# One 128-column weight operand for the adapter's first product, and values without their bias

## The chip, the cores and the metric

The kernel runs on one core of a Trainium2 chip. The metric is the device time of one execution in microseconds (us). A core has TensorE (PE in the profile; its weight loads are PEld), VectorE (DVE), ScalarE (ACT), GpSimd (POOL) and SyncE (SP, which issues most of the DMAs). Each engine runs its own list of instructions in order, and they wait for one another by semaphores. PSUM has eight banks of 128x512 float32 words.

## The reference, cut to what matters

A layer of the macaron kind over a batch of 16 with 512 rows of 256: half a feed-forward block, attention with 16 heads of 16, half a feed-forward block again. In each feed-forward block one of 8 adapters is chosen for each batch, the one whose encoder and decoder rebuild the input best.

```python
# feed-forward, twice for each batch, on x = layernorm(...)
h = relu(einsum('btd,ndh->nbth', x, W_enc) + b_enc)
recon = einsum('nbth,nhd->nbtd', h, W_dec) + b_dec
top1 = argmin(mean((recon - x[None]) ** 2, axis=(2, 3)), axis=0)
adp = connected_idx[top1]
mid = relu(einsum('btd,bdr->btr', x, W_down[adp]) + b_down[adp])   # 256 -> 64
out = x @ W_base + b_base + einsum('btr,brd->btd', mid, W_up[adp]) + b_up[adp]
# attention
q, k, v = x @ Wq + bq, x @ Wk + bk, x @ Wv + bv                    # q and k are rotated
attn = softmax(einsum('bhqd,bhkd->bhqk', q, k) / sqrt(HD))
y = einsum('bhqk,bhkd->bqhd', attn, v).reshape(b, s, D) @ W0 + b0
```

A row of `attn` sums to 1, so a bias on `v` reaches the output as `bv @ W0`, the same for every row.

## The kernel before, in words

Products that need full precision are made from two float32r parts of each operand, a high and a low one: high x high, low x high, high x low, for each of the two 128-row halves `c` of the 256 channels, so six matmuls of 512 columns for one output of 128x512.

The work is a software pipeline over the batches. It is cut into small named stages, and for each engine an order of the stages is written out by hand (`tensor_order`, `scalar_order`, `vector_order`, `gpsimd_order`, `sync_order` for the 13 middle iterations, and a `_begin` and an `_end` for each). In `stage("up", +1, 0, 1)` the numbers are the batch relative to the iteration, the feed-forward block `f` (0 or 1) and a part. In one iteration TensorE computes attention of one batch, and between its pieces the first block of the next batch and the second block of the batches before. The stages that matter here:

- `s1` and `s2` (lines 1680 and 1692): two score matmuls each, into two banks. VectorE takes row maxima of `s1` (line 2076), ScalarE the exponentials of `s2` (line 1919). `pv` (line 1706) multiplies with the values, `nt`, `ot`, `op` (lines 1868, 1876, 1884) finish the attention, `mt` (line 1729) transposes the maxima.
- `tr`, `en`, `gr`, `cost`, `pick`: transposes of the normalised input, the encoder (line 1761, ScalarE's relu in line 1977), the losses (lines 1778 and 1780, VectorE's sum in line 2131; 1789), the choice (VectorE lines 2146 to 2165). GpSimd then copies the chosen weights (lines 2321 to 2326) and counts them on `sel`.
- `dn`: the chosen 256x64 product. TensorE does six matmuls with 64 weight columns (line 1802), ScalarE one relu with the bias (line 1984), counted on `mid_done`.
- `up`: two halves, each twice six matmuls and two with `mid` (lines 1821 and 1822), of which the first waits for `mid_done`. VectorE adds the result to the input (line 2175).
- `qk` and `va`: the projections (lines 1837 and 1847). ScalarE copies queries and keys out with their bias (line 1992), and VectorE the values with theirs (line 2183). Rotation and splitting follow (`ro1`, `ro2`, `ro3` on VectorE, GpSimd and ScalarE), and SyncE sends the parts through HBM into `stack`.

Block 0 of a batch has the banks 6 and 7 (`early`), block 1 the bank 5 (`late`), which it shares with `mt`.

In a middle iteration TensorE's order around the two `dn` is this; block 1's `dn` stands far ahead of its `up`, block 0's close to it:

```python
stage("s2", -1, 14, 0); stage("s1", 0, 3, 0); stage("dn", -2, 1)     # block 1
...
stage("s2", 0, 0, 1); stage("s1", 0, 5, 1); stage("dn", +1, 0)       # block 0
stage("nt", -1, 0); stage("nt", -1, 1)
stage("s2", 0, 1, 0); stage("s1", 0, 6, 0); stage("up", +1, 0, 0)
```

Of the kernel before, what the change touches and what calls it, by code (L numbers as in the profile page):

```python
# [108 lines left out]
def tensor_order(stage):  # L109
# [16 lines left out]
    stage("s1", 0, 2, 0)  # L126
    stage("gr", +1, 0, 0)
# [5 lines left out]
    stage("dn", -2, 1)  # L133
# [9 lines left out]
    stage("cost", +1, 0)  # L143
    stage("s2", -1, 15, 1)
    stage("s1", 0, 4, 1)
    stage("up", -2, 1, 1)
# [16 lines left out]
    stage("s2", 0, 2, 0)  # L163
    stage("ot", -1)
    stage("s1", 0, 7, 0)
# [39 lines left out]
    stage("s2", 0, 7, 1)  # L205
    stage("s1", 0, 12, 1)
    stage("en", -1, 1, 2)
    stage("s2", 0, 8, 0)
    stage("pv", 0, 3)
# [4 lines left out]
    stage("gr", -1, 1, 0)  # L214
    stage("s2", 0, 9, 0)
    stage("tr", +2, 0, 0)
    stage("s1", 0, 14, 0)
    stage("gr", -1, 1, 1)
    stage("s2", 0, 9, 1)
    stage("tr", +2, 0, 1)  # L220
# [11 lines left out]
def tensor_begin(stage):  # L232
# [18 lines left out]
    stage("qk", 0, 0)  # L251
    stage("qk", 0, 1)
    stage("en", 1, 0, 1)
    stage("va", 0, 0)
    stage("va", 0, 1)
    stage("en", 1, 0, 2)
# [10 lines left out]
    stage("s1", 0, 1, 0)  # L267
    stage("dn", 1, 0)
    stage("s1", 0, 1, 1)
    stage("s1", 0, 2, 0)  # L270
    stage("s1", 0, 2, 1)
    stage("up", 1, 0, 0)
    stage("s1", 0, 3, 0)
# [15 lines left out]
    stage("s2", 0, 2, 1)  # L289
    stage("tr", 1, 2, 0)  # L290
    stage("s1", 0, 7, 1)
    stage("s2", 0, 3, 0)
    stage("pv", 0, 0)
    stage("tr", 1, 2, 1)
    stage("mt", 0, 1)
# [3 lines left out]
    stage("s2", 0, 4, 0)  # L299
    stage("s1", 0, 9, 0)  # L300
    stage("pv", 0, 1)
    stage("s2", 0, 4, 1)
    stage("s1", 0, 9, 1)
    stage("qk", 1, 0)
    stage("s2", 0, 5, 0)
    stage("s1", 0, 10, 0)
    stage("qk", 1, 1)
    stage("s2", 0, 5, 1)
    stage("s1", 0, 10, 1)
    stage("s2", 0, 6, 0)  # L310
    stage("va", 1, 0)
    stage("s1", 0, 11, 0)
    stage("pv", 0, 2)
    stage("s2", 0, 6, 1)
    stage("s1", 0, 11, 1)
    stage("va", 1, 1)
    stage("s2", 0, 7, 0)
    stage("s1", 0, 12, 0)
    stage("qk", 1, 2)
    stage("mt", 0, 2)  # L320
    stage("s2", 0, 7, 1)
    stage("qk", 1, 3)
    stage("s1", 0, 12, 1)
    stage("pv", 0, 3)
    stage("s2", 0, 8, 0)
    stage("s1", 0, 13, 0)
    stage("s2", 0, 8, 1)
# [7 lines left out]
    stage("tr", 2, 0, 0)  # L335
    stage("s2", 0, 10, 1)
    stage("s1", 0, 15, 1)
    stage("tr", 2, 0, 1)
# [3 lines left out]
def tensor_end(stage):  # L342

    stage("en", -1, 0, 0)
    stage("mt", -3, 3)
    stage("s2", -3, 11, 0)
# [5 lines left out]
    stage("s2", -3, 12, 0)  # L352
    stage("pv", -3, 5)
    stage("s1", -2, 1, 0)
# [4 lines left out]
    stage("s1", -2, 2, 0)  # L359
    stage("s2", -3, 13, 1)  # L360
    stage("gr", -1, 0, 0)
    stage("s1", -2, 2, 1)
    stage("s2", -3, 14, 0)
    stage("gr", -1, 0, 1)
    stage("s1", -2, 3, 0)
    stage("dn", -4, 1)
    stage("s2", -3, 14, 1)
    stage("s1", -2, 3, 1)
    stage("gr", -1, 0, 2)
    stage("gr", -1, 0, 3)  # L370
    stage("mt", -2, 0)
    stage("pv", -3, 6)
    stage("s2", -3, 15, 0)
    stage("s1", -2, 4, 0)
    stage("up", -4, 1, 0)
    stage("cost", -1, 0)
    stage("s2", -3, 15, 1)
# [3 lines left out]
    stage("s2", -2, 0, 1)  # L381
    stage("pv", -3, 7)
    stage("s1", -2, 5, 1)
    stage("up", -4, 1, 1)
    stage("dn", -1, 0)
    stage("nt", -3, 0)
    stage("nt", -3, 1)
    stage("s2", -2, 1, 0)
    stage("s1", -2, 6, 0)
    stage("up", -1, 0, 0)  # L390
    stage("nt", -3, 2)
    stage("s2", -2, 1, 1)
    stage("nt", -3, 3)
    stage("s1", -2, 6, 1)
    stage("s2", -2, 2, 0)
    stage("up", -1, 0, 1)
# [21 lines left out]
    stage("s1", -2, 9, 1)  # L418
    stage("tr", -3, 1, 1)
    stage("s2", -2, 5, 0)  # L420
# [7 lines left out]
    stage("s2", -2, 6, 1)  # L428
    stage("s1", -2, 11, 1)
    stage("qk", -1, 2)  # L430
    stage("en", -3, 1, 0)
    stage("s2", -2, 7, 0)
    stage("pv", -2, 2)
    stage("s1", -2, 12, 0)
    stage("mt", -2, 2)
    stage("qk", -1, 3)
    stage("s2", -2, 7, 1)
    stage("s1", -2, 12, 1)
    stage("en", -3, 1, 1)
    stage("pv", -2, 3)  # L440
    stage("s2", -2, 8, 0)
    stage("en", -3, 1, 2)
    stage("s1", -2, 13, 0)
    stage("s2", -2, 8, 1)
    stage("en", -3, 1, 3)
    stage("s1", -2, 13, 1)
    stage("s2", -2, 9, 0)
    stage("gr", -3, 1, 0)
# [3 lines left out]
    stage("s1", -2, 14, 1)  # L452
    stage("s2", -2, 10, 0)
    stage("s1", -2, 15, 0)
    stage("gr", -3, 1, 2)
    stage("s2", -2, 10, 1)
    stage("pv", -2, 4)
# [16 lines left out]
    stage("dn", -3, 1)  # L474
    stage("s1", -1, 2, 1)
    stage("s2", -2, 14, 0)
    stage("s1", -1, 3, 0)
    stage("s2", -2, 14, 1)
    stage("s1", -1, 3, 1)
    stage("pv", -2, 6)  # L480
    stage("s2", -2, 15, 0)
    stage("s1", -1, 4, 0)
    stage("mt", -1, 0)
    stage("s2", -2, 15, 1)
    stage("up", -3, 1, 0)
    stage("s1", -1, 4, 1)
    stage("pv", -2, 7)
    stage("up", -3, 1, 1)
    stage("s2", -1, 0, 0)
    stage("s1", -1, 5, 0)  # L490
    stage("nt", -2, 0)
    stage("s2", -1, 0, 1)
    stage("nt", -2, 1)
    stage("s1", -1, 5, 1)
    stage("nt", -2, 2)
    stage("nt", -2, 3)
    stage("s2", -1, 1, 0)
    stage("s1", -1, 6, 0)
    stage("s2", -1, 1, 1)
    stage("s1", -1, 6, 1)  # L500
    stage("s2", -1, 2, 0)
    stage("ot", -2)
    stage("s1", -1, 7, 0)
    stage("pv", -1, 0)
# [4 lines left out]
    stage("op", -2, 1)  # L509
    stage("s1", -1, 8, 0)  # L510
    stage("s2", -1, 3, 1)
    stage("mt", -1, 1)
# [13 lines left out]
    stage("s1", -1, 11, 1)  # L526
    stage("pv", -1, 2)
    stage("s2", -1, 7, 0)
    stage("s1", -1, 12, 0)
    stage("mt", -1, 2)  # L530
    stage("s2", -1, 7, 1)
    stage("s1", -1, 12, 1)
    stage("pv", -1, 3)
# [211 lines left out]


def scalar_end(stage):

    stage("en", -1, 0, 0)
    stage("s2", -3, 11, 0)  # L750
    stage("s2", -3, 11, 1)
# [1612 lines left out]
```

## Time and profile before

| | |
|---|---|
| median of 3 runs | 1786.44 us (1784.21 to 1788.15) |
| the profiled execution | 1784.44 us |
| its span, first to last instruction | 1782.6 us |
| mean granted TensorE clock | 0.988 of full speed |
| PE, DVE, ACT, POOL busy | 1703.6, 1265.2, 973.0, 497.0 us |

The span is 1.8 us shorter than the execution's own time. Matmuls overlap one another in the records: one of 512 columns is shown as some 390 ns long, while the next starts about 230 ns after it. So the cost of a group of matmuls is read from the chain of waits, where pieces follow end to end, and not from the mean of one.

### The profile page before, as it was taken

Reading aid. Unit: us, or ns where it says so; the run is one execution under the profiler, and the core shown is the slowest. Engines: PE = TensorE matmul, PEld = TensorE weight load, DVE = VectorE, ACT = ScalarE, POOL = GpSimd, SP = SyncE. Lnnn points to the kernel's source line nnn. Section 1 sums busy time; section 2 is a strip of 40 time slices with the busy share of each in tenths; the row PEclk is TensorE's granted clock in tenths of the full one; section 3 lists DMA queues with packets and bytes.
Section 4 is the critical chain, followed back from the end, with each engine's and each line's share of the span. In section 5 each row is a group of like instructions: output and inputs, shape, how many; then the busy total and the mean of one; then the engine's idle time right before and its main releaser. Section 6 shows DMA issues by size and latency. Waiting matters only on the chain.

```text
span 1782.6 us, 26353 instructions
## 1 busy us (share of the span) xinstructions
PE 1703.6 (96%) x9064; PEld 997.6 (56%) x9064; DVE 1265.2 (71%) x2829; ACT 973.0 (55%) x1954; POOL 497.0 (28%) x663
## 2 busy tenths in 40 slices
PE   5878999999999999999999999999999999999987
PEld 4624555556565565656556565655656565554345
DVE  6478786867768686776868677686867868576722
ACT  2326474655637465563746556474655647465551
POOL 2314060421406042140604215060421506023010
PEclk9889999999999999999999999999999999999999
DMA  5343342223334222343422234332233434224300
GB/s 133 48 71 72 37 82 32 62 40 60 72 49 79 35 61 42 61 72 48 76 36 62 43 61 72 48 75 36 61 45 60 72 48 75 32 33 70 44 1 24
DMA packets 96715, 99.37 MB, mean 56 GB/s; under 512 B 19972, under 2 KB 88261, under 8 KB 96453
## 3 DMA queue, kind: packets, MB, share of 16 engines
q1 hardware_dynamic: 93830, 97.16, 32.6%
q8 instruction: 72, 1.18, 0.3%
q10 hardware_dynamic: 2752, 0.54, 0.2%
q14 instruction: 61, 0.50, 0.1%
HBM read 63.54 MB, written 33.55 MB: 54 GB/s over the span
## 4 chain that ended last, share of the span: by engine, by line
PE 84%; DVE 8%; ACT 2%; issue 2%; POOL 2%; DMA 1%; SPq 0%; POOLq 0%; ACTq 0%; DVEq 0%
PE ps L1706 11%; PE ps L1692 11%; PE ps L1680 11%; PE ps L1778 10%; PE ps L1761 10%; PE ps L1780 6%; PE ps L1821 5%; PE ps L1837 5%; PE ps L1822 3%; PE ps L1802 3%; PE ps L1745 2%; PE ps L1847 2%; DVE mx L2076 2%; PE ps L1884 2%; PE ps L1868 2%
## 5 line engine op out<-in xcount | busy, mean ns | idle before, releaser
L2076 DVE TENSOR_REDUCE mx<-ps 128x1 f32<-128x512 f32 x1024 | 655.5, 683 | 258.8 <-PE ps L1680 257.6
L1919 ACT ACTIVATE pr<-ps 128x512 f32<-128x512 f32 x1024 | 557.3, 599 | 386.5 <-PE ps L1692 383.0
L1680 PE MATMUL ps<-stack 96*128 96x512 bf16 x1024 | 316.0, 384 | 12.4 <-DVE mx L2076 8.5
L1692 PE MATMUL ps<-stack 98*128 98x512 bf16 x1024 | 314.6, 384 | 9.2 <-ACT pr L1919 3.3
L1706 PE MATMUL ps<-pr,va 128*32 128x512 f32 x2048 | 247.7, 602 | 2.6 <-ACT pr L1919 2.3
L1692 PEld LDWEIGHTS ps<-stack 98*128 98x128 bf16 x1024 | 82.4, 98 | 184.5 <-issue 106.9
L1680 PEld LDWEIGHTS ps<-stack 96*128 96x128 bf16 x1024 | 95.2, 98 | 156.0 <-DVE mx L2076 50.9
L2321 POOL CAST wdh<-wd_all 128x128 fp32r x32 | 9.5, 297 | 585.2 <-DVE adapter L2165 557.4
L2131 DVE SCALAR_TENSOR_TENSOR ps<-ps,wb,h 128x512 f32<-128x512 f32 x128 | 96.5, 755 | 65.1 <-PE ps L1780 65.1
L1780 PE MATMUL ps<-h,gram_w 128*128 128x512 f32 x256 | 130.6, 592 | 0.0
L1706 PEld LDWEIGHTS ps<-pr,va 128*32 128x32 f32 x2048 | 53.7, 109 | 136.2 <-issue 131.2
L1778 PE MATMUL ps<-xh,w_dh 128*128 128x512 f32 x256 | 121.5, 475 | 6.8 <-DVE ps L2131 4.4
L1761 PE MATMUL ps<-xh,w_eh 128*128 128x512 f32 x256 | 123.6, 483 | 0.9 <-DVE xl L2118 0.9
L2248 POOL TENSOR_SCALAR rs<-mv 128x4 f32<-128x4 f32 x48 | 11.4, 237 | 404.7 <-DVE mv L2096 399.6
L1977 ACT ACTIVATE h<-ps,benc 128x512 f32<-128x512 f32 x128 | 87.1, 693 | 64.1 <-PE ps L1761 64.0
L2277 POOL TENSOR_TENSOR qb<-qb,cst 128x512 f32<-128x512 f32 x64 | 91.4, 1428 | 47.4 <-DVE qs L2191 46.9
L1761 PE MATMUL ps<-xl,w_eh 128*128 128x512 f32 x256 | 101.8, 398 | 0.0
L1761 PE MATMUL ps<-xh,w_el 128*128 128x512 f32 x256 | 101.6, 397 | 0.0
L1778 PE MATMUL ps<-xl,w_dh 128*128 128x512 f32 x256 | 101.2, 395 | 0.0
L1778 PE MATMUL ps<-xh,w_dl 128*128 128x512 f32 x256 | 101.1, 395 | 0.0
L2285 POOL TENSOR_TENSOR qb<-qb,parts 128x512 f32<-128x512 f32 x64 | 78.9, 1233 | 79.0 <-ACT parts L1998 79.0
L1821 PE MATMUL ps<-w_bh,xh 128*128 128x256 f32 x256 | 96.4, 376 | 1.5 <-ACT mid L1984 1.5
(153 smaller groups left out, 2951.5 us busy)
## 6 DMA issues: line engine op xcount, KB each, us to landing
stack<-scratch SPq DMA_DIRECT2D x384, 128.0 KB, 6.3
scratch<-parts SPq DMA_DIRECT2D x64, 384.0 KB, 2.6
xin<-in_L_attn_x_dram SPq DMA_DIRECT2D x15, 512.0 KB, 4.0
out_dram<-x SPq DMA_DIRECT2D x15, 512.0 KB, 8.8
stack<-wu_mT SPq DMA_DIRECT2D x128, 4.0 KB, 1.7
cst<-in_const_dram SPq DMA_DIRECT2D x1, 1024.0 KB
raw<-in_L_ffn_W_dec_dram ACTq DMA_DIRECT2D x1, 512.0 KB, 5.6
pr<-in_L_ffn_W_enc_dram SPq DMA_DIRECT2D x2, 256.0 KB, 7.6
```

What stands on the lines that cost most here:

```text
L1680: pe.matmul(bank1[:, t % 2, :], stack[0][0:KB, hd, 128 * t:128 * t + 128], stack[1][0:KB, hd, :], start=True, stop=True).then_inc(s1_full. ...
L1692: pe.matmul(bank2[:, a % 2, :], stack[1][:, 4 * g + a, 128 * t:128 * t + 128], stack[0][:, 4 * g + a, :], start=True, stop=True).then_inc( ...
L1706: last = pe.matmul(bank_o[32 * a:32 * a + 32, :], va[b.odd][:, t, 4 * g + a, :], held(b, n)[:, a, :], start=(t == 0), stop=(t == T - 1))
L1761: last = pe.matmul(bank, w[:, c, 2 * p:2 * p + 2, :].rearrange("p n r -> p (n r)"), x[e][:, c, :], start=(c == 0 and w is w_eh and x is xh ...
L1778: pe.matmul(bank, w[:, c, 128 * p:128 * p + 128], x[e][:, c, :], start=(c == 0 and w is w_dh and x is xh), stop=False)
L1780: pe.matmul(bank, gram_w[:, p, :], h[:, p, :], start=False, stop=True).then_inc(gr_full[f].sem, 1)
L1821: pe.matmul(o, x[e][:, c, 128 * t:128 * t + 128], w[:, c, :], start=(c == 0 and n == 0), stop=False)
L1837: last = pe.matmul(bank, y[:, c, 128 * m:128 * m + 128], x[:, c, :], start=(c == 0 and n == 0), stop=(c == C - 1 and n == 2))
L1919: act.activation(held(b, n)[:, a, :], bank2[:, a % 2, :], ACT.Exp, scale=SCALE).then_inc(ex_done.sem, 1)
L2076: dve.tensor_reduce(mx[:, hd // 4 % 2, e:e + 1], bank1[:, t % 2, :], AX.X, ALU.max).then_inc(mx_done.sem, 1)
L2131: dve.scalar_tensor_tensor(out=bank, in0=bank, scalar=wb2[:, p:p + 1], in1=h[:, p, :], op0=ALU.add, op1=ALU.mult, accum_out=r[e][:, p:p + ...
L2277: pool.tensor_tensor(q[:], q[:], v["cos"][:, S * (k // 2):S * (k // 2) + S], ALU.mult).then_inc(cos_done.sem, 1)
```

## The change

1. `dn`: the high and the low part of the chosen weights lie side by side in one tile `wd`, 128 columns wide. TensorE multiplies it with the high and the low part of the input: four matmuls of 128 columns in place of six of 64. Rows 0 to 63 of the bank then hold the high weights' sum, rows 64 to 127 that of the low weights.
2. The two halves have to be added. ScalarE copies rows 64 to 127 into `mid` (stage `dn`), VectorE adds both and the bias into the bank (a new stage `dn`), and ScalarE does the relu into `mid` (a new stage `ds`).
3. `va`: ScalarE copies the values out, without a bias. Once, at the start, TensorE computes `bv @ W0` (two float32 matmuls of 256 columns ahead of the first `qk`), and VectorE adds it to `b0`. The broadcast load of `bv` becomes two loads of a column.
4. All orders are written anew. Most moves are by one or two places.

```diff
@@ tensor_order (middle iterations)
     stage("s1", 0, 2, 0)
+    stage("dn", -2, 1)
     stage("gr", +1, 0, 0)
...
     stage("s1", 0, 3, 0)
-    stage("dn", -2, 1)
...
     stage("up", -2, 1, 0)
-    stage("cost", +1, 0)
     stage("s2", -1, 15, 1)
     stage("s1", 0, 4, 1)
+    stage("cost", +1, 0)
...
     stage("dn", +1, 0)
+    stage("s2", 0, 1, 0)
+    stage("s1", 0, 6, 0)
     stage("nt", -1, 0)
     stage("nt", -1, 1)
-    stage("s2", 0, 1, 0)
-    stage("s1", 0, 6, 0)
     stage("up", +1, 0, 0)
@@ tensor_end
     stage("op", -1, 1)
     stage("gr", -2, 1, 0)
     stage("gr", -2, 1, 1)
+    stage("tr", -1, 1, 0)
     stage("gr", -2, 1, 2)
-    stage("tr", -1, 1, 0)
     stage("tr", -1, 1, 1)
     stage("gr", -2, 1, 3)
+    stage("en", -1, 1, 0)
     stage("cost", -2, 1)
-    stage("en", -1, 1, 0)
     stage("en", -1, 1, 1)
+    stage("en", -1, 1, 2)
     stage("dn", -2, 1)
-    stage("en", -1, 1, 2)
+    stage("en", -1, 1, 3)
     stage("up", -2, 1, 0)
-    stage("en", -1, 1, 3)
-    stage("up", -2, 1, 1)
@@ scalar_order
+    stage("dn", -2, 1)
     stage("s2", -1, 14, 0)
     stage("pv", -1, 5)
-    stage("dn", -2, 1)
     stage("s2", -1, 14, 1)
+    stage("ds", -2, 1)
...
     stage("s2", 0, 0, 1)
     stage("dn", +1, 0)
+    stage("ds", +1, 0)
     stage("s2", 0, 1, 0)
...
+    stage("ro2", +1, 0)
     stage("tr", -1, 1, 1)
-    stage("ro2", +1, 0)
     stage("s2", 0, 6, 0)
+    stage("va", +1, 0)
     stage("s2", 0, 6, 1)
+    stage("va", +1, 1)
     stage("ro3", +1, 0)
@@ vector_order
+    stage("gr", +1, 0, 2)
+    stage("dn", -2, 1)
     stage("s1", 0, 3, 1)
-    stage("gr", +1, 0, 2)
...
     stage("s1", 0, 5, 1)
+    stage("dn", +1, 0)
     stage("nt", -1, 0)
...
     stage("ro1", +1, 1)
-    stage("va", +1, 0)
     stage("s1", 0, 11, 0)
     stage("s1", 0, 11, 1)
     stage("ms", 0, 2)
-    stage("va", +1, 1)
@@ vector_end
     stage("s1", -2, 6, 0)
+    stage("dn", -1, 0)
     stage("nt", -3, 0)
@@ tensor: down
-                    for w, x in ((wdh, xh), (wdl, xh), (wdh, xl)):
-                        last = pe.matmul(bank[0:R, :], w[e][:, c, :], x[e][:, c, :], ...)
+                    for x in (xh, xl):
+                        last = pe.matmul(bank, wd[e][:, c, :, :].rearrange("p k r -> p (k r)"), x[e][:, c, :], ...)
@@ tensor: project
+                if initial(b) and k == 0:
+                    for c in range(C):
+                        last = pe.matmul(bank_o[:, 0:D], bv_col[:, c:c + 1].to_broadcast([128, 128]), w_0[:, c, :], ...)
+                    last.then_inc(s_wt, 1)
@@ scalar
-                act.activation(mid[e][0:R, :], bank[0:R, :], ACT.Relu, bias=bdn[e][:, 0:1]).then_inc(mid_done[f].sem, 1)
+                act.copy(mid[e][0:R, :], bank[R:2 * R, :]).then_inc(rest_mid[f].sem, 1)
+            def middle_sum(b, f):
+                act.wait_ge(*sum_mid[f].at(b, 0))
+                act.activation(mid[e][0:R, :], bank[0:R, :], ACT.Relu).then_inc(mid_done[f].sem, 1)
+            def values(b, half):
+                act.wait_ge(*va_full.at(b, half))
+                act.copy(va[b.odd][:, 2 * half:2 * half + 2, :, 0:HD], bank...).then_inc(va_done.sem, 1)
@@ vector
+            def down(b, f):
+                dve.wait_ge(*rest_mid[f].at(b, 0))
+                dve.wait_ge(*sel[f].at(b, 1))
+                dve.scalar_tensor_tensor(out=bank[0:R, :], in0=bank[0:R, :], scalar=bdn[e][:, 0:1], in1=mid[e][0:R, :],
+                                         op0=ALU.add, op1=ALU.add).then_inc(sum_mid[f].sem, 1)
-            def values(b, half):   # a tensor_tensor with the broadcast bias
@@ vector: swap, before the first
+                    dve.wait_ge(s_wt, 3)
+                    dve.tensor_tensor(b0_bc[:], b0_bc[:], bank_o[:, 0:D], ALU.add).then_inc(s_ready, 1)
```

## Rows read from the trace of the kernel before

**Rows 1.** The page: busy time by engine, and the chain's shares.

```profile
PE 1703.6 (96%) x9064; PEld 997.6 (56%) x9064; DVE 1265.2 (71%) x2829; ACT 973.0 (55%) x1954; POOL 497.0 (28%) x663
...
PE 84%; DVE 8%; ACT 2%; issue 2%; POOL 2%; DMA 1%; SPq 0%; POOLq 0%; ACTq 0%; DVEq 0%
```

**Rows 2.** Windows: one middle iteration of 104 us.

```profile
core 0: us, PE busy (x) PEld busy (x) DVE busy (x) ACT busy (x) POOL busy (x), PEclk, DMA share, GB/s
...
832.00:936.00 104.00, 103.50 (x566) 61.64 (x565) 77.82 (x174) 60.46 (x122) 30.66 (x41) 1.00 0.33 55
```

**Rows 3.** Chain of waits, 809 to 831 us: start, us, what.

```profile
809.51 1.40 PE ps L1778 x6
...
827.17 1.37 PE ps L1802 x6
828.54 0.87 PE ps L1868 x8
...
830.28 0.71 PE ps L1821 x6
```

**Rows 4.** Instruction groups: busy us, mean ns, idle before.

```profile
L1928 ACT COPY raw<-ps 128x512 f32<-128x512 f32 x64 | 38.3, 599 | 27.7 <-PE ps L1706 27.7
...
L1984 ACT ACTIVATE mid<-ps,bdn 64x512 f32<-64x512 f32 x32 | 21.8, 682 | 75.8 <-PE ps L1802 75.8
L2183 DVE TENSOR_TENSOR va<-ps,bv_bc 128x512 f32<-128x512 f32 x32 | 21.8, 683 | 0.3 <-PE ps L1847 0.3
...
L2175 DVE SCALAR_TENSOR_TENSOR x<-ps,xin 128x512 f32<-128x512 f32 x30 | 20.7, 691 | 30.4 <-PE ps L1822 30.4
```

**Rows 5.** Timelines of ScalarE, VectorE and GpSimd around block 0's `dn`.

```profile
826.75 1.09 ACT L1919 ACTIVATE pr<-ps 128x512 f32<-128x512 f32 x2
828.58 0.68 ACT L1984 ACTIVATE mid<-ps,bdn 64x512 f32<-64x512 f32 x1 [0.74 <-PE ps L1802]
...
826.99 1.29 DVE L2076 TENSOR_REDUCE mx<-ps 128x1 f32<-128x512 f32 x2 [1.54 <-PE ps L1680]
...
825.11 0.39 POOL L2326 COPY wu_mT<-wu_all 65x256 f32 x1
```

**Rows 6.** Chain of waits: the last `dn`.

```profile
1770.10 2.84 PE ps L1802 x6
1772.96 0.69 ACT mid L1984
1773.70 0.98 PE ps L1821 x6
```

**Rows 7.** Instruction groups: weight loads of 64 and of 128 columns.

```profile
L1761 PEld LDWEIGHTS ps<-xh,w_eh 128*128 128x128 f32 x256 | 48.5, 189 | 21.4 <-DVE xl L2118 1.3 <-ACT h L1977 0.9
...
L1802 PEld LDWEIGHTS ps<-xh,wdh 128*64 128x64 f32 x64 | 9.0, 141 | 15.8 <-issue 5.2 <-POOL wu_mT L2326 4.9
```

**Rows 8.** Chain of waits, the first `dn`.

```profile
40.63 2.81 PE ps L1802 x6
43.46 0.69 ACT mid L1984
```

**Rows 9.** Chain of waits in the end: float32 matmuls, and `dn` of batch 14.

```profile
1666.71 1.73 PE ps L1884 x8
...
1746.97 1.59 PE ps L1802 x6
```

**Rows 10.** Waits of the whole run: us in total, times, longest.

```profile
PE ps L1789 <- DVE z L2140: 4.0, 3, 1.4
```

**Rows 11.** Windows and timeline where ScalarE would copy the values.

```profile
855.00:860.00 5.00, 5.00 (x36) 3.97 (x35) 3.79 (x6) 5.00 (x14) 3.31 (x3) 1.00 0.00 0
...
863.52 1.09 ACT L1919 ACTIVATE pr<-ps 128x512 f32<-128x512 f32 x2 [0.91 <-PE ps L1692]
```

**Rows 12.** Waits between 780 and 884 us: TensorE's weight loads for VectorE.

```profile
PEld ps L1680 <- DVE mx L2076: 0.8, 1, 0.8
PEld ps L1778 <- DVE ps L2131: 0.5, 1, 0.5
```

More of the change, by code:

```diff
@@ L827, in scalar_end @@
     stage("s2", -2, 14, 1)
+    stage("dn", -3, 1)
+    stage("ds", -3, 1)
     stage("s2", -2, 15, 0)
@@ L1463, in macaron @@
         zt = [sb(f"zt{f}", [128, C, N]) for f in range(2)]
-        wdh, wdl = ([sb(f"{n}{f}", [128, C, R], FR) for f in range(2)] for n in ("wdh", "wdl"))
+        wd = [sb(f"wd{f}", [128, C, 2, R], FR) for f in range(2)]
         wu_mT = [sb(f"wu_mT{f}", [128, D]) for f in range(2)]
@@ L1555, in macaron @@
         mid_done = [sig(f"mid_done{f}", 1) for f in range(2)]
+        rest_mid = [sig(f"rest_mid{f}", 1) for f in range(2)]
+        sum_mid = [sig(f"sum_mid{f}", 1) for f in range(2)]
         up_done = [sig(f"up_done{f}", 2) for f in range(2)]
@@ L1800, in down @@
                 for c in range(C):
-                    for w, x in ((wdh, xh), (wdl, xh), (wdh, xl)):
-                        last = pe.matmul(bank[0:R, :], w[e][:, c, :], x[e][:, c, :], start=(c == 0 and w is wdh and x is xh),
-                                         stop=(c == C - 1 and x is xl))
+                    for x in (xh, xl):
+                        last = pe.matmul(bank, wd[e][:, c, :, :].rearrange("p k r -> p (k r)"), x[e][:, c, :],
+                                         start=(c == 0 and x is xh), stop=(c == C - 1 and x is xl))
                 last.then_inc(dn_full[f].sem, 1)
@@ L1833, in project @@
                     pe.wait_ge(*va_done.at(b, k - 2))
+                if initial(b) and k == 0:
+                    for c in range(C):
+                        last = pe.matmul(bank_o[:, 0:D], bv_col[:, c:c + 1].to_broadcast([128, 128]), w_0[:, c, :], start=(c == 0),
+                                         stop=(c == C - 1))
+                    last.then_inc(s_wt, 1)
                 w, m = (w_q, w_k)[k % 2], k // 2
@@ L1993, in project @@
                    .then_inc(qb_done.sem, 1)
+            def values(b, half):
+                if half == 0:
+                    act.wait_ge(*pv_done.at(b - 2, G * T // 2 - 1))
+                bank = early[half]
+                act.wait_ge(*va_full.at(b, half))
+                act.copy(va[b.odd][:, 2 * half:2 * half + 2, :, 0:HD], bank.rearrange("p (t h d) -> p t h d", t=2, d=HD))\
+                   .then_inc(va_done.sem, 1)
             def high(b, k):
@@ L2008, in out_transposed @@
                     act.copy(oT[:, c, :], out_bank(b, c)).then_inc(oT_done.sem, 1)
-            do = dict(s2=s2, pv=pv, mt=maxima, lx=normalise, tr=transposed, en=encode, dn=down, qk=project,
+            do = dict(s2=s2, pv=pv, mt=maxima, lx=normalise, tr=transposed, en=encode, dn=down, ds=middle_sum, qk=project, va=values,
                            ro2=high, ro3=middle, ot=out_transposed)
@@ L2167, in choose @@
                     dense_weights()
+            def down(b, f):
+                e = slot(b, f)
+                bank = dense_bank(b, f, 1)
+                dve.wait_ge(*rest_mid[f].at(b, 0))
+                dve.wait_ge(*sel[f].at(b, 1))
+                dve.scalar_tensor_tensor(out=bank[0:R, :], in0=bank[0:R, :], scalar=bdn[e][:, 0:1], in1=mid[e][0:R, :], op0=ALU.add,
+                                         op1=ALU.add).then_inc(sum_mid[f].sem, 1)
             def up(b, f, half):
@@ L2176, in up @@
                                          in1=src[:, q, :], op0=ALU.mult, op1=ALU.add).then_inc(up_done[f].sem, 1)
[L2178 to L2185 removed]
             def swap(b, k):
+                if initial(b) and k == 0:
+                    dve.wait_ge(s_wt, 3)
+                    dve.tensor_tensor(b0_bc[:], b0_bc[:], bank_o[:, 0:D], ALU.add).then_inc(s_ready, 1)
                 dve.wait_ge(*qb_done.at(b, k))
@@ L2223, in out_project @@
                    .then_inc(x2_done.sem, 1)
-            do = dict(s1=s1, ms=split_maxima, st=statistics, lx=normalise, tl=low_part, gr=gram, cost=cost, pick=choose, up=up, va=values,
-                           ro1=swap, ro3=low, nt=natural,
+            do = dict(s1=s1, ms=split_maxima, st=statistics, lx=normalise, tl=low_part, gr=gram, cost=cost, pick=choose, dn=down, up=up, ro1=swap, ro3=low, nt=natural,
                            op=out_project)
```

350 lines of the change are left out of this document (180 added, 170 removed).

## The prediction

> **What bounds the kernel now.** I read the page first. TensorE is busy for 96% of the span and makes up 84% of the chain that ended last, while VectorE is at 71% and ScalarE at 55% [rows 1]. That is an average, so I asked for windows. In a middle iteration TensorE is busy for 103.5 of 104 us, VectorE for 77.8 and ScalarE for 60.5 [rows 2]: there TensorE is the bound, and a matmul less shortens the run by its own spacing, unless TensorE then waits. The spacing has to come from the chain of waits, since the mean of one matmul counts overlap. Six matmuls of `dn` take 1.37 us there and six of 128 columns 1.40, so 0.233 each [rows 3].
>
> **What TensorE saves.** Four matmuls of 0.233 us in place of six that take 1.37: 1.37 - 0.93 = 0.44 us for each of the 32 `dn`. The rest is what else changes around each.
>
> The width costs nothing in that sum, since a load of 128 columns takes 189 ns against 141 [rows 7], under the spacing of 233. The Trainium skill, page TensorE: Matmul & The Clock Gate, section LDWEIGHTS, says that a load's time goes with its columns, and its section Back-to-back issue gap that the spacing is set by load and matmul together. If they simply added up, its figures would give, as an estimate, 6 x (0.216 + 0.053) - 4 x (0.216 + 0.107) = 0.32 us saved in place of 0.44. The trace speaks against adding: twice the columns move the spacing by 4 ns.
>
> **What the halves' sum costs.** Before, `dn` is followed by one relu: it starts 0.04 us after the product's end, takes 0.68 [rows 5], and TensorE can go on 0.05 later [rows 6]. Afterwards there are three steps on two engines: copy on ScalarE, 0.58 (128x512 copies average 0.60 [rows 4]; a lone one is a little shorter), sum on VectorE, 0.69 like line 2175 [rows 4], relu without a bias pointer, 0.60 like the exponentials, of which a pair takes 1.09 [rows 5]. With hand-overs of 0.04, 0.05 and 0.04 that is 2.00 us from the product's end to `mid_done`. No row shows a 64x512 copy from one half of the partitions to the other. From below: if half the rows were to halve each step, 0.29 + 0.35 + 0.30 and the hand-overs make 1.07. From above: each of the three as long as the longest of these rows, 0.69, and 0.15 for each hand-over make 2.5. I take the 2.00, since the old relu on 64 rows took 682 ns, no less than line 2183's sum on 128, so half the rows halve nothing.
>
> Block 1's `dn` has all four `gr` of the next batch behind it before `mt` and `up` need the bank or `mid` (each of them over 1.40 us [rows 3]), and its copy and its relu are put behind work that TensorE does not wait for. So it keeps its 0.44 us. There are 14 of these, batches 0 to 13, in the middle and in the first part of the end: **-6.2 us**. On VectorE the added sum (0.69) and the removed value copies (0.68 each, two for each batch [rows 4]) cancel, since there are two `dn` for each batch.
>
> Block 0's `dn` has little cover. From its end to the first matmul of `up` TensorE does `nt` twice, `s2` and `s1`: 828.54 to 830.28, 1.74 us [rows 3]. The new order permutes these four and has the same 1.74. Before, the 0.77 of the relu lay inside. Afterwards `mid` comes at 2.00, and a matmul that had to wait starts late on top: six of line 1821 take 0.98 us behind such a wait [rows 6] and 0.71 without [rows 3]; with the 0.05 that is 0.32. So TensorE stands still for 2.00 + 0.32 - 1.74 = 0.58 us. Neither engine is late for it: ScalarE's exponentials end at 827.84 and VectorE's maxima at 828.28 [rows 5], while they are wanted from 828.1 and 828.7 (0.44 earlier than `dn` ended before). ScalarE's next exponentials stand behind its relu, and end some 1.1 us after it, while TensorE has half of `up` to do before it needs them, twice 0.71 [rows 3] and the products with `mid`. The chosen weights are there at 825.50 [rows 5], over a us early. So for each of the 13 middle batches 0.58 - 0.44 = +0.14: **+1.8 us**. What block 1 saves, block 0 does not.
>
> Batch 15's block 0, in the end, is worse: there VectorE's order has the two maxima of the `s1` behind `dn` ahead of its sum. They take 1.29 us [rows 5] and can begin some 0.2 after the product's end, so the sum starts 0.8 later than its copy allows, and the stall is about 1.4: 1.4 - 0.44, **+1.0**.
>
> **Start and end.** At the first `dn` nothing covers anything. Six matmuls at the lower clock took 2.81 us with their drain [rows 8], or 0.43 each, so two less save 0.85; the chain behind grows by 2.00 - 0.72 = 1.28. `bv @ W0` stands ahead of the first `qk`: a float32 matmul of 256 columns is spaced 1.73 / 8 = 0.22 [rows 9], twice that at the lower clock, so two cost 0.86. Together **+1.3**. Batch 1's `dn` lies where row maxima bind: -0.85 on TensorE against +0.69 on VectorE, **-0.2**. The two small loads of `bv` I cost at nothing: they stand among the other first loads, and the first `dn`, which waits for the chosen weights, is 40 us away [rows 8]; without that cover they would cost what a queue step takes, well under a us.
>
> In the end, `cost` of batch 14 waited 1.4 us for VectorE [rows 10], and the new order puts an encoder product of 1.40 in there; behind it `dn` still waits for the weights, which come at 1746.97 [rows 9], and `up` then waits for the longer chain, some 0.5 more. The work from there to batch 15's `cost` comes 1.4 - 0.5 earlier: **-0.9**. The last `dn` is bare again: 2.84 / 6 x 2 = 0.95 saved, 1.28 added, **+0.35**.
>
> Sum: -6.2 + 1.8 + 1.0 + 1.3 - 0.2 - 0.9 + 0.35 = **-2.8 us**. The profiled execution took 1784.44 us, 1.8 more than its span, and stands 2.0 below the median of the runs. So 1781.6 for an execution like it, and 1783.6 for the median.
>
> **Rivals.**
> *All hidden.* If the three short steps are near their lower bound, TensorE does not stop in block 0: 13 x 0.58 less, -10.3, 1776. Half the partitions speak for it; the relu's 682 ns on 64 against 599 and more on 128 speaks against.
> *ScalarE becomes the bound where it copies values.* It is busy for 5.00 of 5 us from 855 to 860, and its exponentials have 0.91 us of air only at 863.5 [rows 11]. Two copies of 0.5 to 0.6 fill that, and `s2` needs the banks that they delay. If 0.7 us of the 1.1 reach TensorE in each of 13 iterations, +9.3: 1793, slower. It decides from some 0.5 us for each iteration. Against it: the air of 0.91 us lies just where the first copy goes, and a value copy on ScalarE ends over 2 us before `qk` asks for its bank.
> *VectorE, relieved, stops holding TensorE.* In an iteration the weight loads wait 0.8 us for maxima and 0.5 for the gram's sum [rows 12]. 1.4 us less of value copies where VectorE is busiest could free some 0.4 of it: -5.2, 1778.
> *The narrow product was not dearer.* If four wide matmuls cost nearly what six narrow ones did, by loads that show, the 27 savings in the middle shrink. With 0.12 less each: +3.2, so +0.4, 1787. The rule cited above would lead here. Rows 3 and 7 speak against.
>
> **Numbers.** Forecast 0.45, with a range of its own from 1780 to 1787 (the stall between 0.35 and 0.85 us); all hidden 0.15; ScalarE 0.17; VectorE 0.13; no saving by width 0.10. 0.2% of 1786.4 is 3.6 us, about what a measurement of this kernel tells from no change. Faster, under 1782.9: 0.16 of the forecast's, all of the hidden, 0.12 of VectorE's, 0.43. Slower, over 1790.0: 0.14 of ScalarE's and 0.02 beside, 0.16. Within: 0.41. The range goes from 1775.5, which takes in the lower bound of the chain, to 1791.
>
> **What would show it.** Line 1802's successor: 128 matmuls in fours of 0.93 us. TensorE waiting some 0.4 us, as the records count it, for `mid` ahead of line 1821's block 0, in each middle iteration, and a middle iteration some 0.3 us shorter. If `s2` waits for ScalarE beyond 860, or the waits for maxima are gone, it was a rival. I am wrong if ScalarE's copy or relu takes much less than 0.58, or if one of them comes up behind an exponential.

## The result, and the profile after

The changed kernel takes 1795.89 us (median of 5 runs, 1792.22 to 1797.88) against 1786.44 (5 runs, 1784.02 to 1788.49): ratio 1.0059, 95% interval [1.0048, 1.0071]. It is slower by about 10 us, where 3 us less was forecast.

The page of the kernel after, which answers to [rows 1]:

```profile
PE 1706.9 (95%) x9004; PEld 998.8 (56%) x9004; DVE 1279.5 (71%) x2830; ACT 1010.4 (56%) x2018; POOL 494.1 (28%) x663
...
PE 73%; DVE 16%; ACT 5%; issue 3%; POOL 3%; DMA 1%; POOLq 0%; ACTq 0%; DVEq 0%; SPq 0%
```

The busy shares hardly move. The chain does: TensorE's part falls from 84% to 73%, VectorE's doubles to 16%. Something on VectorE is now late for TensorE.

The chain of waits around block 0's `dn` in a middle iteration, which answers to [rows 3]:

```profile
833.56 0.94 PE ps L1824 x4
834.50 0.02 issue
834.52 0.59 ACT mid L2010
835.11 0.03 issue
835.14 0.76 DVE ps L2214
835.90 0.02 issue
835.92 0.60 ACT mid L2016
836.52 0.04 issue
836.57 0.98 PE ps L1843 x6
```

The four wide products take 0.94 us, and `mid` comes 2.02 us behind them. That is the forecast, almost to the hundredth (0.93 and 2.00). So the loss is elsewhere.

To find it I use one measure in all that follows: the **distance**, from one batch's first score product to the next batch's. Each batch has 64 of them, so the first is every 64th record of that line. The timelines of before and after at batches 3 and 7:

```profile
375.24 0.60 PE L1680 MATMUL ps<-stack 96*128 96x512 bf16 x2
791.62 0.60 PE L1680 MATMUL ps<-stack 96*128 96x512 bf16 x2
```

```profile
380.08 0.60 PE L1700 MATMUL ps<-stack 96*128 96x512 bf16 x2
798.41 0.60 PE L1700 MATMUL ps<-stack 96*128 96x512 bf16 x2
```

A quarter of the difference is 104.10 us before and 104.58 after. The eleven distances from batch 2 to batch 13 agree within 0.1 us but for one or two (their median: 104.09 and 104.60), so a tenth of a microsecond can be read there, where whole runs scatter by several. The 11.5 us between the two spans are made up so: up to batch 1's first scores 3.4, from there to batch 2's 1.1, batches 2 to 13 4.9, 13 to 14 1.9, 14 to 15 -0.5, the rest 0.6.

Where VectorE is late, about 85 us into such an iteration, its timeline after:

```profile
883.37 1.28 DVE L2116 TENSOR_REDUCE mx<-ps 128x1 f32<-128x512 f32 x2
884.57 2.57 DVE L2149 SCALAR_TENSOR_TENSOR xn<-xin,mv,rs 128x256 f32<-128x256 f32 x4
887.06 1.28 DVE L2116 TENSOR_REDUCE mx<-ps 128x1 f32<-128x512 f32 x2
888.26 0.74 DVE L2171 SCALAR_TENSOR_TENSOR ps<-ps,wb,h 128x512 f32<-128x512 f32 x1
```

And the same place before:

```profile
876.88 1.66 DVE L2109 SCALAR_TENSOR_TENSOR xn<-xin,mv,rs 128x256 f32<-128x256 f32 x4
```

The four operations that normalise the next batch, `lx(+2,0)`, took 1.66 us before and take 2.57 after, though nothing in them was changed, and VectorE has no idle time right behind them in which to catch up. GpSimd at that time, after and before:

```profile
885.43 1.42 POOL L2328 TENSOR_TENSOR qb<-qb,parts 128x512 f32<-128x512 f32 x1 [1.70 <-ACT parts L2038]
```

```profile
878.57 1.17 POOL L2285 TENSOR_TENSOR qb<-qb,parts 128x512 f32<-128x512 f32 x1 [2.51 <-ACT parts L1998]
```

The waits of TensorE's weight loads for VectorE in that iteration, which answer to [rows 12]:

```profile
PEld ps L1700 <- DVE mx L2116: 1.9, 4, 0.8
...
PEld ps L1800 <- DVE ps L2171: 1.2, 2, 0.6
```

That is 3.1 us where it was 1.3. As to what changed: before, GpSimd's subtraction for the third rotated projection, its stage `ro2(+1,2)`, starts when the four have ended. After, it starts in the middle of them. It waits for ScalarE's copy, the stage of the same name there, here after and before:

```profile
884.75 0.61 ACT L2038 CAST parts<-qb 128x512 bf16<-128x512 f32 x1
```

```profile
877.89 0.61 ACT L1998 CAST parts<-qb 128x512 bf16<-128x512 f32 x1
```

Counted from the iteration's first score product (798.41 and 791.62), that copy starts at the same time in both, 86.3 us. It is VectorE that comes to its four operations 0.9 us later, at 86.2 in place of 85.3.

### The profile page after: what moved, and what is told of

Read it like the earlier page. It is cut to its first block, busy times and chain, and to the rows that moved or that the text cites. A ratio compares the mean times of both kernels' runs of the same rounds, so it can differ in the third digit from the quotient of the medians.

```text
span 1794.1 us, 26301 instructions
## 1 busy us (share of the span) xinstructions
PE 1706.9 (95%) x9004; PEld 998.8 (56%) x9004; DVE 1279.5 (71%) x2830; ACT 1010.4 (56%) x2018; POOL 494.1 (28%) x663
## 4 chain that ended last, share of the span: by engine, by line
PE 73%; DVE 16%; ACT 5%; issue 3%; POOL 3%; DMA 1%; POOLq 0%; ACTq 0%; DVEq 0%; SPq 0%
PE ps L1728 10%; PE ps L1800 9%; PE ps L1712 9%; PE ps L1700 9%; PE ps L1783 7%; PE ps L1843 6%; PE ps L1802 5%; DVE mx L2116 5%; PE ps L1864 4%; PE ps L1844 3%; DVE xn L2149 3%; PE ps L1874 2%; PE ps L1767 2%; PE ps L1824 2%; ACT pr L1946 2%
## 5 line engine op out<-in xcount | busy, mean ns | idle before, releaser
L1700 PE MATMUL ps<-stack 96*128 96x512 bf16 x1024 | 320.4, 385 | 10.8 <-DVE mx L2116 8.7
L2364 POOL CAST wd<-wd_all 128x128 fp32r x32 | 9.5, 296 | 570.9 <-DVE adapter L2205 434.5
L2320 POOL TENSOR_TENSOR qb<-qb,cst 128x512 f32<-128x512 f32 x64 | 100.9, 1576 | 140.4 <-DVE qs L2233 140.4
```

What stands on the lines that cost most here:

```text
L1700: pe.matmul(bank1[:, t % 2, :], stack[0][0:KB, hd, 128 * t:128 * t + 128], stack[1][0:KB, hd, :], start=True, stop=True).then_inc(s1_full. ...
L2320: pool.tensor_tensor(q[:], q[:], v["cos"][:, S * (k // 2):S * (k // 2) + S], ALU.mult).then_inc(cos_done.sem, 1)
```

## The experiments

Each is compared with the kernel before, run beside it on the same chip. The ratio comes from all its runs; the distance (within 0.02 us of the median over batches 2 to 13) and the start of batch 1's first score product come from one profiled execution each.

| kernel | distance, us | batch 1's first scores at, us | ratio to before, 95% interval |
|---|---|---|---|
| before | 104.09 | 171.7 | |
| changed | 104.58 | 175.1 | 1.0059 [1.0048, 1.0071] |
| down projection alone | 103.80 | 179.5 | 1.0033 [1.0019, 1.0047] |
| values alone | 104.00 | 177.6 | 1.0019 [1.0007, 1.0032] |
| orders alone | 104.97 | 174.4 | 1.0060 [1.0042, 1.0077] |
| changed, `ro2(+1,1)` first | 104.54 | 171.1 | 1.0032 [1.0018, 1.0046] |
| both parts, old orders | 103.75 | 175.6 | 1.0048 [1.0036, 1.0060] |
| the same, other bank | 103.20 | 181.4 | 1.0004 [0.9992, 1.0015] |
| changed, two copies first | 104.52 | 171.0 | 1.0051 [1.0038, 1.0064] |
| before, two copies late | 104.77 | 176.0 | 1.0050 [1.0037, 1.0063] |
| other bank, new start | 103.20 | 177.3 | 0.9980 [0.9971, 0.9990] |
| changed, copies and encoder | 103.94 | 171.1 | 0.9983 [0.9973, 0.9993] |
| changed, `ro2(+1,2)` later | 103.94 | 172.6 | 0.9974 [0.9962, 0.9987] |
| before, encoder early | 105.53 | 169.4 | 1.0108 [1.0087, 1.0128] |
| changed, later, other bank | 103.41 | 172.4 | 0.9949 [0.9932, 0.9967] |
| other bank, new start and end | 103.20 | 170.9 | 0.9929 [0.9911, 0.9948] |
| before, `ro2(+1,2)` later | 104.09 | 178.6 | 1.0002 [0.9986, 1.0017] |

### Taking the change apart

The down projection alone: the new functions for `dn` and `ds` in the kernel before, the new steps put into its orders at their places, as

```
     stage("s1", 0, 3, 1)
+    stage("dn", -2, 1)      # VectorE
...
     stage("dn", +1, 0)
+    stage("ds", +1, 0)      # ScalarE
```

> The kernel before with the new down projection alone (four 128-column products, the low half copied by ScalarE, the sum on VectorE, the ReLU on ScalarE), the values left on VectorE and the order of the kernel before kept but for the new steps. Theory A, that the new orders hold the loss and the arithmetic does not: the iteration gains 0.87 us of TensorE work and loses 0.6 us at block 0's up projection, 0.2 to 0.3 us for each of 13 batches, against 1 to 2 us at the start and the end, so 1783 to 1787 us (ratio 0.998 to 1.000). Theory B, that the two new VectorE and ScalarE steps themselves delay the maxima and the exponentials: +0.4 us or more for each batch, 1791 us or more (ratio over 1.003).

The values alone: ScalarE's copies put ahead of and behind `s2(0,6,1)`, the bias by way of the output bias.

> The kernel before with the value part alone: values copied by ScalarE, the value bias taken through the output bias, the old down projection and the old order but for the two copies. Theory A: only the start pays (the product of the value bias with W0, 1.6 us, and the wait of the third projection for ScalarE's copy), so +1 to +4 us, 1787 to 1790 us. Theory B, that ScalarE becomes late with its other copies through the two value copies and drags the low parts on GpSimd and VectorE: +0.5 to +0.8 us in each of 13 iterations as well, 1794 to 1799 us.

The orders alone: the new orders, without their new steps, over the old functions.

> The arithmetic of the kernel before (six 64-column products, one ReLU, values on VectorE) walked in the orders of the changed kernel, with VectorE's value steps at their old neighbours. Theory A: the orders alone bring the 0.8 us for each of 13 iterations that the trace of the changed kernel shows ahead of the second decoder's products and at the maxima, so +6 to +11 us, 1792 to 1798 us. Theory B, that the loss comes with the new operations and not with where the stages stand: within 2 us of the kernel before.

Measured: distances of 103.80, 104.00 and 104.97. The down projection gains 0.29 us in an iteration and the values 0.09; the orders lose 0.88, the same sum as the 0.49 by which the changed kernel is longer (0.88 - 0.29 - 0.09 = 0.50). Theory A holds for the iteration. It missed the time of the first kernel, though (1792.75 us, where it had up to 1787), and the second, at 1790.1, is at its upper end: both are slower than before. In their traces batch 1's first scores come 7.8 and 5.9 us later than before, and the stretch from batch 15's first scores to the end is 5.0 and 2.2 us longer (159.7 and 156.8 in place of 154.7). So both ends of the run pay; see the clock below.

Both parts in the old orders, all new steps where the first two kernels have them:

> Both parts of the change (the new down projection and the values on ScalarE) in the orders of the kernel before, with the new steps put in at their places. The three runs so far put 0.88 us of a middle iteration on the orders, 0.30 us of gain on the down projection and 0.08 us of gain on the values. If these add up (theory A), the distance between the scores of two batches is 103.7 us (before 104.09, changed 104.57) and 13 iterations gain 5 us against the kernel before; the start costs 3 to 8 us, by how long TensorE is granted half the clock between 90 and 130 us, so 1785 to 1790 us (ratio 1.000 to 1.002). If the parts disturb each other (theory B), the distance is 104.1 us or more and the time 1793 us or more.

103.75: it adds up. The time, 1793.2 us, does not follow: in the trace the start costs 3.9 us and the stretch behind batch 15's first scores 4.8.

### What in the orders

The first suspicion was one line of ScalarE's order:

```
+    stage("ro2", +1, 1)
     stage("s2", 0, 7, 0)
-    stage("ro2", +1, 1)
```

> The changed kernel with one line moved: ScalarE's first-part copy of the second rotated projection, ro2(+1,1), stands ahead of s2(0,7,0) again as it did before, not behind it. Theory A: that late copy pushes GpSimd's rotation work onto VectorE's four normalising operations, which slow from 0.41 us to 0.64 us each beside it and make VectorE late for the second decoder; with the copy back, 0.5 to 0.8 us for each of 13 iterations return, so 6 to 10 us under the changed kernel: ratio to the kernel before 1.000 to 1.003. Theory B, that the delay has another source (the value copies, or the new steps): the ratio stays at 1.005 to 1.007.

The distance is 104.54: this theory, as put, fell. The run as a whole was 4 us shorter, but that is its start, and who looks at the ratio alone is misled. Its trace has the four operations at 2.58 us still, and VectorE waiting 1.2 us for `ro3(+1,1)`, the next copy. So:

```
+    stage("ro2", +1, 1)
     stage("s2", 0, 7, 0)
-    stage("ro2", +1, 1)
     stage("qk", +1, 2)
+    stage("ro3", +1, 1)
     stage("en", -1, 1, 1)
-    stage("ro3", +1, 1)
```

> The changed kernel with two lines of ScalarE's order moved back: ro2(+1,1) ahead of s2(0,7,0), and ro3(+1,1) ahead of en(-1,1,1). Moving the first alone left the iteration at 104.55 us, and the trace of it still has VectorE wait 1.2 us for ScalarE's second-part copy, ro3(+1,1), which stands behind the encoder step. Theory A: that copy is what is late; GpSimd's rotation then falls on VectorE's four normalising operations (2.6 us in place of 1.7), and with the copy back the wait of the second decoder's products for VectorE (0.46 us more than before) goes: 104.0 to 104.2 us for each iteration, 5 to 7 us off the changed kernel's iterations. Theory B, that the place of TensorE's and VectorE's stages does it: it stays at 104.5 us.

104.52: still not. But the opposite, the kernel before with these two lines as the changed one has them, is slower at once:

> The kernel before with only those two lines of ScalarE's order as the changed kernel has them: ro2(+1,1) behind s2(0,7,0), ro3(+1,1) behind en(-1,1,1). Theory A: the wait and the slower normalising operations appear in the kernel before as well, and its iteration goes from 104.09 to 104.4 or more, so 4 us or more, 1790 us. Theory B: it stays within 0.1 us of 104.09.

104.77, and the mean of the normalising operation goes from 474 to 670 ns (692 in the changed kernel). The group of it in this kernel:

```profile
L2109 DVE SCALAR_TENSOR_TENSOR xn<-xin,mv,rs 128x256 f32<-128x256 f32 x60 | 36.7, 670 | 1.8 <-POOL rs L2250 1.8
```

These two lines are enough to make the loss, and not enough to take it away: there is a second cause with the same effect. In the trace of the changed kernel with both copies first, VectorE waits for TensorE ahead of the maxima of `s1(0,12,1)`, since the new order has `en(-1,1,2)` in front of it. Moving that as well:

```
-    stage("en", -1, 1, 2)
     stage("s1", 0, 12, 1)
-    stage("pv", 0, 3)
+    stage("en", -1, 1, 2)
     stage("s2", 0, 8, 0)
+    stage("pv", 0, 3)
```

> The changed kernel with ScalarE's ro2(+1,1) and ro3(+1,1) ahead as before, and on TensorE the third encoder product en(-1,1,2) behind s1(0,12,1) again and pv(0,3) behind s2(0,8,0). With ScalarE's two alone the iteration stayed at 104.51 us, and VectorE's maximum of s1(0,12,1) came 0.9 us later than in the kernel before, after a wait for TensorE. Theory A, that either of the two delays alone is enough to put the four normalising operations beside GpSimd's subtraction: now the operations take 1.7 us again, the wait of the second decoder's products goes, and the iteration is 104.0 to 104.2 us. Theory B: 104.4 us or more.

103.94, the operations at 478 ns again, and 1782.6 us. Whether TensorE's two lines alone would have done it in the changed kernel was not tried. In the kernel before, the encoder's move alone (with `pv`) does something else:

> The kernel before with two stages of TensorE's order as the changed kernel has them: en(-1,1,2) ahead of s1(0,12,1), and pv(0,3) ahead of s2(0,8,0). Theory A, that this too makes VectorE late enough for the slow normalising operations: 104.4 to 104.8 us for an iteration in place of 104.09. Theory B: within 0.1 us of 104.09.

105.53, but with the normalising operations at 478 ns: theory A was wrong about how. There ScalarE's copy `ro2(+1,2)` is late too: it starts at 885.65, when the four operations (883.98, 1.66 us) are over. What costs is that `en(-1,1,3)` waits 1.7 us for ScalarE's `h`, which is behind exponentials whose scores TensorE, in this order, delivers later. Out of the waits of one iteration of it:

```profile
PEld ps L1761 <- ACT h L1977: 1.7, 1, 1.7
```

A stage moved in one engine's order alone can cost more than the whole change.

### The collision by itself

If the loss is that GpSimd's subtraction and VectorE's four operations fall together, then it must help to make the subtraction later. In the changed kernel, one line of ScalarE's order:

```
-    stage("ro2", +1, 2)
     stage("s2", 0, 8, 1)
+    stage("ro2", +1, 2)
```

> The changed kernel with one copy of ScalarE made later: the first part of the third rotated projection, ro2(+1,2), stands behind the exponentials of s2(0,8,1) and not ahead of them, so GpSimd's subtraction that waits for it starts some 1.1 us later. Theory A, that VectorE's four normalising operations are slow (2.6 us in place of 1.7) because they run beside that subtraction: they end before it starts and take 1.7 to 2.0 us, the wait of the second decoder's products shrinks, and the iteration falls from 104.57 us to 104.1 to 104.3 although an operation was delayed. Theory B, that the delay of VectorE's queue has nothing to do with GpSimd: nothing gained, 104.6 us or more.

VectorE and GpSimd in its trace:

```profile
878.22 1.66 DVE L2149 SCALAR_TENSOR_TENSOR xn<-xin,mv,rs 128x256 f32<-128x256 f32 x4
```

```profile
880.07 1.16 POOL L2328 TENSOR_TENSOR qb<-qb,parts 128x512 f32<-128x512 f32 x1 [2.68 <-ACT parts L2038]
```

The four end at 879.88 and the subtraction starts at 880.07. They take 1.66 us, the distance is 103.94, and the kernel takes 1782.35 us, 13.5 under the changed one, though nothing but one copy was made later. Between the two traces the span is 13.4 us shorter. The distances give 9.2 of that (6.9 from batch 2 to 13, 0.6 ahead of them, 1.7 between 13 and 14). The rest is where nothing was touched: 2.5 up to batch 1's first scores and 1.7 behind batch 15's. It could be that the move is good in itself; so the kernel before, which has no such collision, with the same move:

> The kernel before with the same single move, ro2(+1,2) behind s2(0,8,1). In it the four normalising operations already end before GpSimd's subtraction starts and take 1.7 us. Theory A, that the move helps only where the two fall together: no gain, 104.1 us for an iteration (or up to 0.1 more), 1785 to 1787 us. Theory B, that the move gives something of its own, and the changed kernel's gain of 13.5 us by it says nothing of a collision: 103.5 us or less, 1779 us or less.

104.09, and 1.0002. The move gives nothing where there is nothing to part.

How the two engines meet shows in one answer for the four operations after:

```profile
L2149 DVE SCALAR_TENSOR_TENSOR xn<-xin,mv,rs x4: 473/478/1385, 884.6 to 885.7; 128x256 f32<-128x256 f32 x4
```

Three take their usual 473 to 478 ns. Only the last, which starts at 885.75 while the subtraction runs from 885.43 to 886.85, takes 1385: it ends 0.28 us after the subtraction does. So it is in each of the 13 middle iterations: it ends 0.28 to 0.29 us after the subtraction. That is an operation held up until the other ends, not one slowed all along. The subtraction is longer too, 1.42 us in place of 1.17; it started inside the third of the four. The Trainium skill, page SBUF — State Buffer, section Who interferes with whom, says this: a VectorE instruction with two inputs in SBUF and a GpSimd instruction that reads SBUF take the same ports, the one that starts first has them for its whole length, and the other stands still. The trace agrees: this operation reads `xin` and `rs` there, both in SBUF, and GpSimd's subtraction had started 0.32 us ahead of it. The maxima that follow, with one input and that from PSUM, run beside GpSimd's next operation in their usual 1.28 us for two.

### The wait that was forecast, taken away

Block 0's `dn` filled the bank that `up` fills next, so `up` could not start ahead of `mid`. The output accumulator's bank is free at that time:

```
+            return dense_bank(b, f, 1) if f or initial(b) else bank_o
...
+                if not f:
+                    pe.wait_ge(*raw_done.at(b - 2, G - 1))
...
+                    if t == 0 and not (f or initial(b)):
+                        pe.wait_ge(*mid_done[f].at(b, 0))
                     last = pe.matmul(o, mid[e][:, 128 * t:128 * t + 128], wu[e], start=False, stop=True)
```

> The kernel of both parts in the old orders, with block 0's down projection of every batch but the first written into the output accumulator's bank, which is free there, in place of the bank that the up projection fills; so the up projection starts its twelve base products at once and waits for the ReLU only ahead of its first product with the hidden layer. Theory A, that the 0.6 us stall at the up projection is the price of the added sum: it goes, the distance between batches falls from 103.7 to 103.1 us, 13 iterations give 8 us, 1777 to 1783 us (ratio 0.995 to 0.999). Theory B, that the time is set there by VectorE's or ScalarE's exponentials and maxima and the stall is only where TensorE shows it: the distance stays at 103.6 us or more.

103.20 in place of 103.75: the 0.59 us wait goes, nearly whole, and 1793.2 us become 1785.8. This is level with before only. Its trace, one of its longest runs (1790.98 us), gains 11.8 us from batch 1 to batch 14 and loses 9.7 ahead of that and 8.7 behind batch 15's first scores. The start first, with the changed kernel's orders:

> The kernel with both parts in the old orders and block 0's down projection in the output accumulator's bank, its start walked in the changed kernel's orders. With the old start TensorE was granted half the clock for 30.7 us on end from about 91 to 97 us (kernels of the values alone, of both parts, and of this bank); the changed kernel's start had 6.8 and 10.2 us in its trace. Theory A, that the order of the start decides this: the second batch's scores start at 171 to 175 us and not at 182, the iterations stay at 103.2 us, so 1775 to 1781 us, faster than both kernels (ratio 0.995 to 0.998). Theory B, that chance decides it (the kernel before has runs at 1784 and at 1791 us): the same 1786 us as with the old start, give or take 3.

1782.2, between the two ranges: the start gives some of it. With the changed kernel's orders of the end, which cover the last three batches, as well:

> The kernel with both parts, the down projection in the output accumulator's bank, and the middle iterations in the order of the kernel before, now with the changed kernel's orders for both the start and the end. With the old end orders it took 1782.2 us although its iterations were 103.2 us; from the last score to the end of the span it took 74.5 us against 71.6 us where the changed kernel's end order is used. Theory A, that the end order I made by putting the new steps into the old one costs this: 3 to 5 us less, 1777 to 1780 us. Theory B, that the difference is the clock's: no change beyond 1 us.

1773.0 us, 9 less; more than either theory gave. In the two traces it is 1.2 us between batch 14's and batch 15's first scores and 8.5 from there to the end of the span (163.9 against 155.4). (The traces also differ by 6.5 us up to batch 1's first scores, though the start is the same code: the first of them is the longest of its 12 runs.) So the orders of the end that I had made by putting new steps into the old ones did cost several microseconds, and the changed kernel's own end was the better one. In part it may be the clock again: behind batch 15's first scores TensorE has half of it for 22.8 us against 15.9; which of the two brought the other is not shown. And the other way to it, the changed kernel with both repairs:

> The changed kernel with ro2(+1,2) behind s2(0,8,1) and block 0's down projection in the output accumulator's bank, the up projection waiting for the hidden layer only ahead of its first product with it. With the first alone the iteration is 103.94 us, of which 0.59 us is the up projection's wait. Theory A, that the two losses (VectorE's operations beside GpSimd, and the wait that the sum brings) are independent: 103.3 to 103.4 us for an iteration, 13 times 0.6 us under the 1782.4 us of the first alone, so 1773 to 1777 us (ratio 0.993 to 0.996). Theory B, that the work only queues up at the next limit (VectorE's maxima): 103.7 us or more and 1779 us or more.

103.41 and 1775.0 us: the two losses are independent. This kernel and the one above it are faster than the kernel before by 0.5% and 0.7%.

### The start and TensorE's clock

Windows of 4 us in the kernel before, where TensorE waits for the first projections to come back through memory, and starts the scores (the column behind POOL is the granted clock):

```profile
88.00:92.00 4.00, 0.64 (x3) 0.14 (x2) 2.32 (x11) 0.00 (x0) 0.00 (x0) 0.82 1.15 136
...
96.00:100.00 4.00, 4.00 (x10) 1.51 (x9) 1.57 (x4) 0.67 (x2) 0.35 (x1) 0.50 0.00 0
...
104.00:108.00 4.00, 2.84 (x18) 1.88 (x17) 2.87 (x5) 0.00 (x0) 0.07 (x1) 1.00 0.00 0
```

And in the kernel with the values alone:

```profile
88.00:92.00 4.00, 1.16 (x5) 0.26 (x4) 2.48 (x12) 0.00 (x0) 0.00 (x0) 1.00 0.98 171
...
104.00:108.00 4.00, 3.47 (x12) 1.93 (x10) 1.71 (x3) 0.00 (x0) 0.00 (x0) 0.50 0.00 0
...
116.00:120.00 4.00, 2.84 (x7) 0.52 (x7) 3.39 (x8) 1.09 (x2) 0.50 (x1) 0.50 0.78 134
```

In both the clock falls to half, 1.2 GHz, after TensorE was busy for little of 4 us, 0.64 and 1.16. Before, it is back at 2.4 by 104 us; with the values alone it is at half from 93.5 to 124.2. From batch 0's first scores to batch 1's the kernel before takes 78.9 us and this one 85.8. The kernel before does it too, at times: 7 of its 29 runs beside the first four experiments took over 1790 us, at a mean clock of 0.981 to 0.983, where most of the others took 1783 to 1786 at 0.988 to 0.990. All 12 runs of the down projection alone had 0.978 to 0.982. The kernel before with `ro2(+1,2)` later shows what such a run looks like: its trace is of one that took 1792.45 us, its distances are those of before, and it is 6.9 us longer from batch 0's first scores to batch 1's, with the clock at half from 90.7 to 124.8 us. So the parts put into the old start nearly always end up in the longer case: three of the four traces with new parts in it take over 85 us there, one 82.2. The nine traces with the changed kernel's start take 79.0 to 82.1; why was not tried.

## Why the prediction was wrong, step by step

- **What TensorE saves** (0.44 us for each `dn`): right, 0.94 us for four.
- **The chain of the halves' sum** (2.00 us): right, 2.02. Copy 0.58 and relu 0.59 on average as forecast, the sum 0.75 in place of 0.69.
- **Block 0's stall** (0.58): right, 0.59 (0.32 idle, and 0.27 by which the six products behind the wait take longer, 0.98 against 0.71); TensorE's work between the two ends was the same in the new order. With it fell the rival in which all is hidden, and with the 0.94 the one in which the width costs.
- **A middle iteration 0.3 us shorter**: right for the arithmetic, by 0.29 in the old orders, with another 0.09 by the values. Of the rivals, ScalarE did not become the bound where it copies the values (1793 us, near the result, but for another reason; 13 times 0.7 is 9.1 there, not 9.3), and VectorE's relief was not worth its 0.4.
- **The orders, which the sum has at nothing: the step that failed.** I took the diff of the orders for permutations to be followed only around `dn` ("The new order permutes these four and has the same 1.74") and never priced the rest. They cost 0.88 us in each middle iteration, over 10 us in all, of which 0.64 (104.58 - 103.94) are the collision of `lx(+2,0)` with GpSimd's `ro2(+1,2)`. It also takes 1.7 of the 1.9 us more between batches 13 and 14 (106.1, and 104.3 with the later copy). The other 0.24 of the 0.88 shows as short waits for the row maxima at other places (from batch 7's first scores to batch 8's 1.5 us with the later copy, 0.8 with both parts in the old orders), which I have not traced to a line. With 13 times 0.88 in it the sum of the prediction would have come to 8.6 us more than before, where 9.5 were measured; as its start and its end missed by microseconds as well, that nearness is partly luck.
- **The start** (+1.3): the first `dn` chain grew by the forecast amount (from its first product to `up` 3.6 us before, 4.1 after). `bv @ W0` takes 1.62 us, not 0.86: it has four records of 0.40 at the lower clock, and I had counted two of 0.43. What the start did beyond that is not in the sum at all: in the traces batch 1's first scores come from 2.3 us earlier to 9.7 us later than before, by the clock and by when batch 0's first scores can start. The latter alone is 96.1 us in the changed kernel's trace and 90.6 with `ro2(+1,1)` first, which is the same code up to there.
- **The end** (-0.9 and +0.35): +0.6 from batch 15's first scores on, with the clock at half for 17.2 us of it where it was 9.2. Batch 15's block 0 (+1.0) can't be told from the rest; the stretch that holds it became 0.5 shorter.
- **Range and chances**: 1795.9 lies above 1791, and slower had 0.16. No rival had a mechanism for a kernel in which every piece costs what it should and the queues between them meet differently.

## What to carry to other kernels

A diff that re-plans the order of five queues is a change of its own, and the bigger one: price it apart from the arithmetic, above all for operations of VectorE with two inputs in SBUF that come near GpSimd's, whose start depends on a third engine (here an order that let VectorE come 0.9 us later was enough). Such a collision is found by an operation whose duration changed though its code did not, and proved by making the other one later. In a pipelined kernel compare distances between equal events of successive iterations: they showed 0.1 us where whole runs scatter by 8.

## What the runs showed of the hardware that was not expected

One VectorE operation of 478 ns took 1385 ns when it started inside a GpSimd operation of 1.42 us, and ended 0.28 us after it, while its three neighbours kept their time.

Small operations meet GpSimd in the same way, and one such meeting stands in both kernels. The maxima of 16 columns are split by a cast and a subtraction. Before and after, for one of the four splits of an iteration:

```profile
865.36 1.06 DVE L2082 CAST mx_id<-mx 128x16 bf16<-128x16 f32 x1
866.45 0.18 DVE L2084 TENSOR_TENSOR mx_id<-mx,mx_id 128x16 bf16<-128x16 f32 x1
```

```profile
872.12 0.17 DVE L2122 CAST mx_id<-mx 128x16 bf16<-128x16 f32 x1
872.33 1.21 DVE L2124 TENSOR_TENSOR mx_id<-mx,mx_id 128x16 bf16<-128x16 f32 x1
```

Before, it is the cast, with its one input, that is held up by a GpSimd addition of 1.29 us; after, it is the subtraction. Each ends 0.03 us after GpSimd's operation. The two together take 1.24 us and 1.38, so this is no new loss; who looks at the subtraction alone, 0.18 and 1.21, would think so.

And the kernel before, on one chip, takes 1783 or 1792 us, at a mean granted clock of 0.989 or 0.982. Two traces with the same distances, of 1784.44 and 1792.45 us, have TensorE at half its clock for 17.0 and 34.1 us between 90 and 125 us.
